# A graph kernel of two normalised layers: ten gather-free runs of tiles in place of nine in its second pass

## The chip, the cores and the metric

The kernel runs on one NeuronCore of a Trainium2 chip. The metric is the device time of one execution in microseconds (us), lower is better; it is given as the median of several runs.

The engines are called as in the profile: PE does matrix products (PEld is its weight load), DVE and ACT work on elements, POOL here only issues gathers (indirect DMAs), and SP issues the other DMAs. They run their own instruction lists in order and wait for each other by semaphores only.

## The reference

There are 6250 nodes with 128 features (`x`), 100000 edges sorted by destination (`src`, `dst`), an edge feature matrix `edge_attr` of 100000 x 128 and an edge weight. Cut to what matters:

```python
x = layernorm(x + sigmoid(gcn(relu(gcn(x, W1, b1)), W2, b2)))  # self-loops, symmetric norm
z, rh = x @ fc_w.T, edge_attr @ fc_r_w.T
e = leaky_relu(z[src] @ a0 + z[dst] @ a1 + rh @ a2)
alpha = segment_softmax(e, dst)
agg = segment_sum(alpha * (z[src] + rh), dst)
x = layernorm(x + relu(agg + z @ loop_w))
```

A `gcn` multiplies rows by a weight, gathers them by `src`, scales them per edge and sums them by `dst`.

## The kernel before

The edges lie in 782 tiles of 128 edges, in 98 groups of eight tiles. Since `dst` is sorted, the destinations of a tile fall into a window of 128 nodes. For a tile, POOL gathers the 128 source rows into a ring in on-chip memory (L720, one indirect DMA for each tile), DVE builds a matrix `S` that holds each edge's weight in the column of its destination (`build_S`, L1608), and PE multiplies rows by `S` and adds the product to a bank of accumulators (`sum_group`, L858). There are 17 banks of three 128-node blocks (`NA`); when the last group of a bank has been summed, ACT copies the bank out (L1215), PE multiplies it by the layer's weight (`layer`, L932), and DVE and ACT finish its nodes and store their rows for the next pass.

There are three passes over the edges: pass 0 (first GCN layer, reads `x1_d`), pass 1 (second GCN layer, reads `h1_d`) and pass 2 (attention, reads `x2_d`). The gathers of a pass can begin only when the last rows of the pass before are in memory (POOL waits for `h1_stored`, then for `x2_stored`). The ring has 18 places for groups in passes 0 and 1, so POOL can run up to 18 groups ahead of PE.

Some runs of 32 tiles have no gathers. The source rows of all nodes lie on chip anyway (`rows`, 49 blocks of 128). For such a set of 32 tiles the edges are sorted by source block once, in pass 0 (`make_hi`, `make_ranks`, `unpack` on DVE, `count_before`, `permute`, `turn_low` on PE, `store_low` on ACT). Then a run over the set goes through 49 buckets, one for each source block. ACT makes a one-hot of the source's place in its block (`slot_onehot`, L1239 and L1241), PE multiplies it by the block (`look_up`, L898), ACT copies the found rows (`copy_looked`, L1232), DVE builds a matrix of weights and destinations for each bucket (`make_slots`, L1682), and PE sums (`sum_slots`, L910). Four buckets make a chunk, so a run has 13 chunks (`NC`). At the end ACT copies the sum of the set (`copy_set`, L1256) and PE adds it to its bank (`add_sets`, L919).

Nine sets are sorted (`NSET`), one every six steps of pass 0 (`MAKE`). Pass 0 uses six of them, pass 1 all nine (`USED`). That leaves 74 groups (steps) with gathers in pass 0 and 62 in pass 1. The order of each engine's work is written out by hand per step: `CHUNK_AT` lists the step at which each chunk starts, `MAKE` that of each sort, `CLOSEH` the step at which each bank closes. In pass 1 a step of PE is: `look_up` for the chunks of the step before, `pick` (scores of the destinations, two groups in a step by `picks_at`), `add_sets`, `sum_group`, `sum_slots` for the same chunks, `layer`. A step of DVE is: `build_S`, `hidden2` of a bank closed two steps ago, `begin_pick`, `make_slots`, `residual`, then `normal`, `dst_scores` and `node_table` of a bank closed three steps ago. A step of ACT is: copies of the chunks, the copy of a finished set, one-hots for the chunks of the step, `squash` and `spread` of a bank (sigmoid and square root), the bank's copy. `residual` waits for `squash`. On SP's queue two steps before the end of pass 1 there stand four loads of `dlo_d` (L568), three of `edge_attr` (L505) and thirteen of `x2_d` (L574), and behind them the last three stores of `x2_d` (L603).

Of the kernel before, what the change touches and what calls it, by code (L numbers as in the profile page):

```python
# [12 lines left out]
P = 128  # L13
# [4 lines left out]
TC = G * GT  # L18
# [83 lines left out]
SETK = (6, 8, 10, 12, 14, 15, 2, 4, 9)  # L102
USED = ((0, 1, 2, 3, 4, 5), (6, 7, 0, 1, 8, 2, 3, 4, 5))
# [15 lines left out]
NQ = 15  # L119
assert all(bank_of(t0) == bank_of(t0 + ST - 1) == k and column(t0) + SPAN <= BW for k, t0 in zip(SETK, SAT))  # L120
CHUNK_AT = [[29 + m * 40 // (N0 * NC) for m in range(N0 * NC)], [1 + m * 57 // (len(USED[1]) * NC) for m in range(len(USED[1]) * NC)]]
MAKE = [17 + 6 * i for i in range(NSET)]
# [30 lines left out]
def picks_at(h):  # L153

    first = done = 0
    for i in range(h + 1):
        ready = sum(len(node_tiles(k)) // GT for k in range(NA) if CLOSEH[1][k] + 4 <= i)
        first, done = done, max(done, min(ready // 2 * 2, done + 2)) if i < HS[1] - 6 else done
    return range(first, done)
# [78 lines left out]
def build(nc, x, src, dst, edge_attr, edge_weight, W1, b1, W2, b2, fc_w, fc_r_w, attn_w, loop_w, out):  # L238
    ctx = ExitStack()
    with ctx:  # L240
# [61 lines left out]
        cols = sb("cols", [P, max(2 * TC + 2, 2 * SPAN + 2 * NSET * NB)])  # L302
        ewP = cols[:, 0:TC * 3 // 2].bitcast(BF16).rearrange("p (t k) -> p t k", k=3)
        eC, alC = cols[:, 0:TC + 2], cols[:, TC + 2:2 * TC + 2]
        setsum = cols[:, 0:2 * SPAN].rearrange("p (a n) -> p a n", a=2)
        slotD, slotW = (cols[:, 2 * SPAN + k * NSET * NB:2 * SPAN + (k + 1) * NSET * NB].rearrange("p (s a) -> p s a", a=NB) for k in range(2))
# [40 lines left out]
        Lb = sb("Lb", [P, 5, BW])  # L347
        aggT, u = Lb[:, 0:2], Lb[:, 2:4]
# [406 lines left out]
        def _(pe):  # L755
# [157 lines left out]
            def add_sets(p, h):  # L913
                for i in range(p * N0, p * N0 + len(USED[p])):
                    k = SETK[RUNS[i]]
                    if CLOSEH[p][k] == h:
                        pe.wait_ge(s("set_copied"), i + 1)
                        at = column(SAT[RUNS[i]])
                        nc.tensor.matmul(ps[(p * NA + k) % 2][:, at:at + SPAN], ident[:, :], setsum[:, i % 2, :], start=False, stop=False  # L919
                                         ).then_inc(s("set_added"), 1)  # L920
# [31 lines left out]
            for h in range(HS[0]):  # L952
                if h + 1 < R0:
                    lookup(h + 1)
                for s_, g in made_at(h, 2):
                    permute(s_, g)
                for m in chunks_at(0, h - 1):
                    look_up(m)
                for s_, g in made_at(h, 3):
                    if g == ST // GT - 1:  # L960
                        turn_low(s_)
                add_sets(0, h)
                sum_group(0, h)
# [212 lines left out]
        def _(act):  # L1176
# [74 lines left out]
            def copy_set(i):  # L1251
                act.wait_ge(s("slot_summed"), NB * (i + 1))
                if i >= 2:
                    act.wait_ge(s("set_added"), i - 1)
                at = act.value_load(shift[0:1, RUNS[i]:RUNS[i] + 1], min_val=0, max_val=SLACK)
                nc.scalar.copy(setsum[:, i % 2, :], ps[5][:, bass.ds(at, SPAN)]).then_inc(s("set_copied"), 1)  # L1256

            def set_copies(p, h):
                for m in chunks_at(p, h - 1):
                    copy_looked(m)  # L1260
                for m in chunks_at(p, h - 1):
                    if m % NC == NC - 1:
                        copy_set(m // NC)
# [10 lines left out]
            for h in range(HS[0]):  # L1274
                set_copies(0, h)
                for m in chunks_at(0, h):
                    slot_onehot(m)
                for s_, g in made_at(h, 3):
# [21 lines left out]
            for h in range(HS[1]):  # L1300
                set_copies(1, h)
                for m in chunks_at(1, h):
                    slot_onehot(m)
# [160 lines left out]
        def _(dve):  # L1464
# [263 lines left out]
            for h in range(HS[0]):  # L1728
# [4 lines left out]
                for s_, g in made_at(h, 0):  # L1733
                    make_hi(s_, g)
# [4 lines left out]
                for m in chunks_at(0, h):  # L1739
                    make_slots(m)  # L1740
                for s_, g in made_at(h, 2):
                    if g == ST // GT - 1:
                        unpack(s_)
                for k in range(NA):
                    if CLOSEH[0][k] == h - 2:
                        hidden(k)
# [96 lines left out]
            link(v.tensor_scalar(later, iota[:, 0:16], sd[:, 0:1], None, ALU.is_gt))  # L1843
            for h in range(HS[1]):
                build_S(1, h, ewC)
# [11 lines left out]
                for k in range(NA):  # L1857
                    if CLOSEH[1][k] == h - 2:
                        residual(k)
                    if CLOSEH[1][k] == h - 3 and k < NA - 3:  # L1860
                        normal(k)
                        dst_scores(k)
                        node_table(k)
# [11 lines left out]
            for i in range(REST, G // 2):  # L1875
                for k in (NA - 3, NA - 2, NA - 1):
# [385 lines left out]
```

## Time and profile before

| | us |
|---|---|
| median of 3 runs | 2372.62 (2370.83 to 2375.32) |
| the profiled execution's own time | 2381.5 |
| its span in the trace | 2379.7 |
| mean granted clock of TensorE | 0.88 of full speed |
| busy over the span: PE, DVE, POOL, ACT | 77%, 76%, 74%, 40% |

The span is what the trace covers; the profiled execution took 1.8 us more than it, and 8.9 us more than the median. In the trace the first gather of pass 1 starts at 788.76 us, the first of pass 2 at 1439.09 us. Shares over the whole span mix stages with different limits, so the rows below are cut by stage. The time of a gather on POOL is that of its issue; its landing is a DMA.

### The profile page before, as it was taken

To read this page: it belongs to the slowest core of one execution; us is meant where nothing else is said; L and a number is where in the kernel's file an instruction comes from. 1 tells how busy PE (TensorE), PEld (TensorE's weight loads), DVE (VectorE), ACT (ScalarE), POOL (GpSimd) and SP (SyncE) were. 2 spreads that over 40 slices of the span, in tenths; PEclk is the share of its full clock that TensorE was granted. 3 is DMA by queue.
4 is the path that set the end of the run, shared out by engine and by line. 5 is a ranking of instruction groups with operands and counts; after the bars stand their busy time and mean duration, and the time that the engine had idled before them with its cause. 6 is when DMAs were issued, how large, how long until landed. Compare 5 with 4: busy or idle time off the path is not lost.

```text
span 2379.7 us, 40822 instructions
## 1 busy us (share of the span) xinstructions
PE 1827.2 (77%) x13384; PEld 1615.7 (68%) x13384; DVE 1816.9 (76%) x7005; ACT 946.1 (40%) x1754; POOL 1756.1 (74%) x1781
## 2 busy tenths in 40 slices
PE   5657869999998588888889873477776779668976
PEld 4557758788887467777777762467665668657866
DVE  7989979999997356878878857486565876486686
ACT  5740024343432244354454431115562367226721
POOL 7777777777777677777777766777777777777771
PEclk9878889999999799999999985778897889779988
DMA  5243223332333333444545467534455555545550
GB/s 145 60 131 98 60 67 80 81 80 73 83 84 102 95 81 100 123 128 118 137 116 147 141 161 203 140 96 127 117 132 143 131 128 139 142 125 145 132 138 20
DMA packets 272093, 270.54 MB, mean 114 GB/s; under 512 B 43454, under 2 KB 218709, under 8 KB 271862
## 3 DMA queue, kind: packets, MB, share of 16 engines
q1 hardware_dynamic: 201790, 143.87, 21.5%
q0 software_dynamic: 56640, 117.52, 20.7%
q10 hardware_dynamic: 13448, 6.47, 1.0%
q8 instruction: 112, 1.84, 0.3%
q14 instruction: 103, 0.84, 0.1%
HBM read 254.14 MB, written 13.97 MB: 113 GB/s over the span
## 4 chain that ended last, share of the span: by engine, by line
POOL 42%; issue 19%; DVE 18%; PE 11%; DMA 6%; ACT 2%; SPq 2%; ACTq 0%; DVEq 0%; POOLq 0%
POOL ring L720 42%; DVE SR L1608 4%; DVE SR L1571 4%; PE ps L858 3%; DMA ring<-x_d,srcC 2%; PE ps L910 2%; DMA ring<-h_d,srcC 2%; PE ps L860 1%; DVE U L1710 1%; DMA ring<-in_edge_attr_dram 1%; PE ps L898 1%; PE ps L1045 1%; DVE SR L1682 1%; DVE U L1972 0%; SPq L574 0%
## 5 line engine op out<-in xcount | busy, mean ns | idle before, releaser
L720 POOL DMA_INDIRECT ring<-x_d,srcC x1132 | 1130.8, 999 | 369.0 <-issue 359.1
L858 PE MATMUL ps<-SR,ring 128*128 128x128 f32 x3540 | 615.3, 305 | 132.9 <-DVE SR L1608 59.4
L858 PEld LDWEIGHTS ps<-SR,ring 128*128 128x128 f32 x3540 | 536.3, 218 | 158.7 <-issue 94.6
L720 POOL DMA_INDIRECT ring<-h_d,srcC x494 | 477.9, 968 | 158.0 <-issue 153.7
L1682 DVE TENSOR_SCALAR SR<-iota_r,cols 128x288 f32<-128x288 f32 x735 | 364.0, 562 | 62.4 <-PE ps L910 62.0
L910 PE MATMUL ps<-SR 128*128 128x288 f32 x1470 | 379.6, 411 | 0.0
L860 PE MATMUL ps<-SR 128*128 128x128 f32 x1564 | 321.4, 301 | 6.0 <-DVE SR L1608 6.0
L910 PEld LDWEIGHTS ps<-SR 128*128 128x128 f32 x1470 | 275.3, 193 | 71.7 <-issue 2.6
L1232 ACT COPY SR<-ps 128x512 f32<-128x512 f32 (+1 forms) x195 | 107.8, 561 | 473.8 <-PE ps L898 446.4
L860 PEld LDWEIGHTS ps<-SR 128*128 128x128 f32 x1564 | 264.0, 218 | 6.2 <-issue 6.1
L1608 DVE TENSOR_SCALAR SR<-iota,rankC,ewC 128x128 f32<-128x128 f32 x940 | 255.9, 365 | 2.2 <-DVE U L1814 0.6
L1608 DVE TENSOR_SCALAR SR<-iota,rankC,cols 128x128 f32<-128x128 f32 x782 | 209.9, 357 | 5.9 <-PE ps L860 4.3
L898 PE MATMUL ps<-rows,SR 128*128 128x128 f32 x1470 | 187.5, 280 | 17.6 <-ACT SR L1241 14.2
L898 PEld LDWEIGHTS ps<-rows,SR 128*128 128x128 f32 x1470 | 179.5, 195 | 25.6 <-ACT SR L1241 20.0
L720 POOL DMA_INDIRECT ring<-in_x_dram,srcC x144 | 145.4, 1010 | 46.8 <-issue 43.6
L1710 DVE SCALAR_TENSOR_TENSOR U<-SR,v2B 128x128 f32<-128x128 f32 x686 | 152.2, 285 | 6.8 <-DMA SR<-in_edge_attr_dram 5.3
L1239 ACT ACTIVATE SR<-SR,negp 128x512 bf16<-128x512 bf16 (+1 forms) x195 | 134.7, 691 | 27.4 <-PE ps L898 16.9
L1241 ACT ACTIVATE SR<-SR,negp 128x512 f32<-128x512 bf16 (+1 forms) x195 | 136.0, 697 | 6.3
L1919 DVE TENSOR_TENSOR cols<-ring,s1C 128x32 f32<-128x32 f32 (+6 forms) x31 | 5.3, 190 | 149.5 <-DMA ring<-x_d,srcC 149.0
L995 PE MATMUL ps<-ident,cols 128*32 128x128 f32 (+2 forms) x81 | 18.2, 350 | 126.6 <-DVE cols L1922 110.1
L792 PE MATMUL ps<-iota_r,zero_h 1*128 1x512 bf16 (+1 forms) x128 | 50.6, 417 | 72.2 <-DMA ring<-h_d,srcC 22.6
L1352 ACT ACTIVATE U<-U 32x384 f32<-32x384 f32 (+2 forms) x27 | 14.1, 523 | 227.9 <-DVE U L1967 227.7
(288 smaller groups left out, 2716.8 us busy)
## 6 DMA issues: line engine op xcount, KB each, us to landing
SR<-in_edge_attr_dram SPq DMA_DIRECT2D x97, 512.0 KB, 4.1
SR<-low_d SPq DMA_DIRECT2D x90, 256.0 KB
U<-dlo_d SPq DMA_DIRECT2D x74, 256.0 KB
ring<-x_d,srcC POOLq DMA_INDIRECT x1132
ring<-h_d,srcC POOLq DMA_INDIRECT x494
SR<-dlo_d SPq DMA_DIRECT2D x12, 512.0 KB, 6.0
ring<-in_edge_attr_dram SPq DMA_DIRECT2D x12, 512.0 KB
U<-lo_d SPq DMA_DIRECT2D x18, 256.0 KB
```

The costliest lines, as they stand in the source:

```text
L720: pool.indirect_dma_start(ring[:, ring_at(p, h if p < 2 else q), k, 0:width], None, (x if p == 0 and h < R0 else table)[:, :], bass.Indire ...
L858: last = nc.tensor.matmul(ps[(p * NA + k) % 2][:, at], ring[:, ring_at(p, h), j, 0:D], S[:, gg % NS, j, :], start=False, stop=stop)
L860: last = nc.tensor.matmul(ps[2 + k % 2][:, at], rh[:, q % NR, j, :], S[:, gg % NS, j, :], start=False, stop=stop)
L898: last = nc.tensor.matmul(ps[3 + m % 2][:, i * P:(i + 1) * P], ohS[:, m % 2, i * P:(i + 1) * P], rows[:, a, 0:D], start=True, stop=True)
L910: nc.tensor.matmul(ps[5][:, SLACK:SPAN], rowX[:, m % 2, i * P:(i + 1) * P], slotS[:, n % NQ, :], start=False, stop=a == NB - 1).then_inc(s ...
L1232: nc.scalar.copy(rowX[:, m % 2, 0:n], ps[3 + m % 2][:, 0:n]).then_inc(s("looked_copied"), 1)
L1239: nc.scalar.activation(low, low, ACT.Abs, bias=negp[:, 0:1]).then_inc(s("low_apart"), 1)
L1241: return nc.scalar.activation(out, low, ACT.Relu, bias=negp[:, 1:2], scale=-1.0)
L1571: last = v.tensor_scalar(SH[:, q % ND, j, :], iota_h[:, :], rankC[:, t:t + 1], None, ALU.is_equal)
L1608: last = v.tensor_scalar(S[:, gg % NS, j, :], iota[:, :], rankC[:, t:t + 1], w[:, t:t + 1], ALU.is_equal, ALU.mult)
L1682: v.tensor_scalar(slotS[:, n % NQ, :], iota_up, slotD[:, RUNS[i], a:a + 1], slotW[:, RUNS[i], a:a + 1], ALU.is_equal, ALU.mult).then_inc(s ...
L1710: v.scalar_tensor_tensor(junk[:, n % NJ, :], attr, 1.0, v2B[:, :], ALU.mult, ALU.mult, accum_out=s2C[:, t:t + 1]).then_inc(s("rh_dotted"), 1)
```

## The change

Pass 1 runs ten sets without gathers in place of nine; a tenth set is therefore sorted in pass 0, and the sorts follow each other every 5 or 6 steps. Pass 1 then has 58 steps with gathers in place of 62, and its 130 chunks start at `1 + m*5//12` in place of 117 at `1 + m*57//117`. The one-hots for a chunk's lookup are made right behind the copy of the chunk two before it, and no longer behind the copy of a finished set. In pass 1 DVE builds `S` one step ahead. In pass 0 DVE's order within a step changes, and a set's last transposition and store come a step earlier. The ring of bucket matrices has 16 places in place of 15; the second buffer of the set sums moves to `Lb`, for which its first use waits on a store of `dlo_d`. Where more than 12 groups of picks are due, four are done in a step; 35 pairs of picks in place of 36 fall into pass 1, and the node table of bank 13 moves behind the pass.

```diff
-SETK = (6, 8, 10, 12, 14, 15, 2, 4, 9)
-USED = ((0, 1, 2, 3, 4, 5), (6, 7, 0, 1, 8, 2, 3, 4, 5))
+SETK = (6, 8, 10, 12, 14, 15, 2, 3, 4, 11)
+USED = ((0, 1, 2, 3, 4, 5), (6, 7, 8, 0, 1, 2, 9, 3, 4, 5))
-NQ = 15
+NQ = 16
-CHUNK_AT = [[29 + m * 40 // (N0 * NC) for m in range(N0 * NC)], [1 + m * 57 // (len(USED[1]) * NC) for m in range(len(USED[1]) * NC)]]
-MAKE = [17 + 6 * i for i in range(NSET)]
+CHUNK_AT = [[29 + m * 40 // (N0 * NC) for m in range(N0 * NC)], [1 + m * 5 // 12 for m in range(len(USED[1]) * NC)]]
+MAKE = [17 + 11 * i // 2 for i in range(NSET)]
...
-        first, done = done, max(done, min(ready // 2 * 2, done + 2)) if i < HS[1] - 6 else done
+        first, done = done, max(done, min(ready // 2 * 2, done + (4 if ready - done > 12 else 2))) if i < HS[1] - 6 else done
...
+        setsum = (cols[:, 0:SPAN], Lb[:, 4, P:P + SPAN])
...
-                for s_, g in made_at(h, 3):
+                add_sets(0, h)
+                sum_group(0, h)
+                for s_, g in made_at(h, 2):
                     if g == ST // GT - 1:
                         turn_low(s_)
-                add_sets(0, h)
-                sum_group(0, h)
...
+                if i == 1:
+                    act.wait_ge(s("dlo_stored"), 16)
...
                 for m in chunks_at(p, h - 1):
                     copy_looked(m)
+                    if m + 2 < (len(RUNS) if p else N0) * NC:
+                        slot_onehot(m + 2)
...
             for h in range(HS[1]):
                 set_copies(1, h)
-                for m in chunks_at(1, h):
-                    slot_onehot(m)
+                if h == CHUNK_AT[1][0]:
+                    slot_onehot(N0 * NC)
+                    slot_onehot(N0 * NC + 1)
...
+            build_S(1, 0, ewC)
             for h in range(HS[1]):
-                build_S(1, h, ewC)
+                if h + 1 < HS[1]:
+                    build_S(1, h + 1, ewC)
...
-                        node_table(k)
+                        if k < NA - 4:
+                            node_table(k)
...
-                for k in (NA - 3, NA - 2, NA - 1):
+                for k in (NA - 4, NA - 3, NA - 2, NA - 1):
```

In pass 0 `make_hi` moves behind `build_S` and `make_ranks`, `make_slots` behind `unpack`, ACT's one-hots go the same way as in pass 1, and `store_low` follows `turn_low` to `made_at(h, 2)`.

## Rows read from the trace of the kernel before

**Rows 1.** Chain of waits by line from 787, 1195 and 1450 us on.

```profile
by line: POOL ring L720 64.1%; issue 27.7%; DMA ring<-h_d,srcC 8.9%; POOLq L719 0.0%
...
by line: PE ps L910 20.0%; PE ps L858 14.2%; PE ps L898 8.0%; DVE SR L1608 7.9%; DVE SR L1682 5.7%; issue 5.5%; SPq L505 4.1%; SPq L574 3.7%; ACT SR L1239 3.5%; DMA U<-dlo_d 2.5%; PE ps L840 2.4%; ACT L1293 1.7%; ACT SR L1241 1.6%; DVE U L1
...
by line: POOL ring L720 65.3%; issue 25.5%; DMA ring<-x_d,srcC 3.7%; PE ps L858 1.5%; PE ps L860 1.3%; PE ps L1020 0.9%; PE ps L995 0.3%; DVE U L1966 0.2%; DVE U L1972 0.2%; DVE U L1965 0.2%; PE ps L792 0.2%; PE ps L1077 0.1%; DVE U L1973 0
```

**Rows 2.** Busy us of PE, PEld, DVE, ACT, POOL (instructions); clock, DMA, GB/s.

```profile
400.00:500.00 100.00, 93.06 (x629) 81.08 (x630) 92.47 (x271) 41.12 (x71) 77.13 (x76) 0.98 0.31 79
...
787.00:1425.00 638.00, 526.96 (x3601) 458.25 (x3601) 477.48 (x1573) 280.67 (x441) 477.95 (x494) 0.93 0.45 122
```

**Rows 3.** Timeline of POOL: start, length, line, idle before it.

```profile
788.76 0.95 POOL L720 DMA_INDIRECT ring<-h_d,srcC  x1 [7.32 <-issue]
...
1416.41 0.95 POOL L720 DMA_INDIRECT ring<-h_d,srcC  x1 [0.31 <-issue]
1439.09 1.10 POOL L720 DMA_INDIRECT ring<-x_d,srcC  x1 [21.73 <-issue]
```

**Rows 4.** Groups of POOL, 400:700 and 900:1300 us: busy, mean ns, idle.

```profile
L720 POOL DMA_INDIRECT ring<-x_d,srcC x230 | 230.7, 1003 | 70.1 <-issue 67.7 <-DMA ring<-x_d,srcC 2.4
...
L720 POOL DMA_INDIRECT ring<-h_d,srcC x314 | 305.5, 973 | 95.8 <-issue 93.6 <-DMA ring<-h_d,srcC 2.1
```

**Rows 5.** Waits of PE, 787:1425 us: total us, times, longest.

```profile
PE ps L858 <- DVE SR L1608: 32.1, 17, 3.5
PE ps L792 <- DMA ring<-h_d,srcC: 22.6, 5, 14.7
PE ps L858 <- DMA ring<-h_d,srcC: 21.4, 13, 5.2
PE ps L792 <- DVE SR L1608: 15.1, 6, 6.7
PE ps L898 <- ACT SR L1241: 12.0, 9, 2.6
...
PE ps L898 <- ACT SR L1232: 3.3, 3, 1.3
```

**Rows 6.** Columns as rows 2: PE L910, L898, L858, DVE L1682, L1608 alone.

```profile
787.00:1425.00 638.00, 228.54 (x882) 166.23 (x882) 0.93 0.45 122
...
787.00:1425.00 638.00, 112.38 (x882) 108.96 (x882) 0.93 0.45 122
...
787.00:1425.00 638.00, 145.12 (x988) 136.00 (x988) 0.93 0.45 122
...
787.00:1425.00 638.00, 218.74 (x441) 0.93 0.45 122
...
787.00:1425.00 638.00, 133.84 (x494) 0.93 0.45 122
```

**Rows 7.** Timeline of PE at three moments of pass 1.

```profile
1017.39 1.13 PE L898 MATMUL ps<-rows,SR 128*128 128x128 f32 x8 [1.22 <-ACT SR L1232]
...
1346.67 3.64 PE L858 MATMUL ps<-SR,ring 128*128 128x128 f32 x16 [3.49 <-DVE SR L1608]
...
1374.39 2.03 PE L858 MATMUL ps<-SR,ring 128*128 128x128 f32 x16
```

**Rows 8.** Groups of the sorts on DVE and PE, 290:787 us.

```profile
L1649 DVE TENSOR_SCALAR U<-iota,U 128x128 f32<-128x128 f32 x248 | 52.1, 298 | 4.6 <-PE ps L885 4.2
L1637 DVE TENSOR_REDUCE U<-U 128x49 f32<-128x392 bf16 x23 | 24.4, 1061 | 0.8
...
L1635 DVE TENSOR_REDUCE U<-U 128x8 f32<-128x392 f32 x30 | 16.8, 561 | 1.0
...
L885 PE MATMUL ps<-U 128*128 128x98 f32 x498 | 62.2, 279 | 0.7 <-DVE U L1651 0.6
```

**Rows 9.** End of pass 1: timeline of the SP queue and DVE.

```profile
1427.71 9.38 SPq L603 DMA_DIRECT2D x_d<-U  x3
...
1432.65 0.35 DVE L1757 SCALAR_TENSOR_TENSOR U<-ps,dinv,b2B 128x128 f32<-128x128 f32 x1 [7.46 <-DMA x_d<-U]
```

More of the change, by code:

```diff
@@ L301, in build @@
         wraw = s1C[:, 0:R0 * GT]
-        cols = sb("cols", [P, max(2 * TC + 2, 2 * SPAN + 2 * NSET * NB)])
+        cols = sb("cols", [P, max(2 * TC + 2, SPAN + 2 * NSET * NB)])
         ewP = cols[:, 0:TC * 3 // 2].bitcast(BF16).rearrange("p (t k) -> p t k", k=3)
         eC, alC = cols[:, 0:TC + 2], cols[:, TC + 2:2 * TC + 2]
-        setsum = cols[:, 0:2 * SPAN].rearrange("p (a n) -> p a n", a=2)
-        slotD, slotW = (cols[:, 2 * SPAN + k * NSET * NB:2 * SPAN + (k + 1) * NSET * NB].rearrange("p (s a) -> p s a", a=NB) for k in range(2))
+        slotD, slotW = (cols[:, SPAN + k * NSET * NB:SPAN + (k + 1) * NSET * NB].rearrange("p (s a) -> p s a", a=NB) for k in range(2))
         U = sb("U", [P, 4648])
@@ L918, in add_sets @@
                         at = column(SAT[RUNS[i]])
-                        nc.tensor.matmul(ps[(p * NA + k) % 2][:, at:at + SPAN], ident[:, :], setsum[:, i % 2, :], start=False, stop=False
+                        nc.tensor.matmul(ps[(p * NA + k) % 2][:, at:at + SPAN], ident[:, :], setsum[i % 2], start=False, stop=False
                                          ).then_inc(s("set_added"), 1)
@@ L1254, in copy_set @@
                     act.wait_ge(s("set_added"), i - 1)
+                if i == 1:
+                    act.wait_ge(s("dlo_stored"), 16)
                 at = act.value_load(shift[0:1, RUNS[i]:RUNS[i] + 1], min_val=0, max_val=SLACK)
-                nc.scalar.copy(setsum[:, i % 2, :], ps[5][:, bass.ds(at, SPAN)]).then_inc(s("set_copied"), 1)
+                nc.scalar.copy(setsum[i % 2], ps[5][:, bass.ds(at, SPAN)]).then_inc(s("set_copied"), 1)
             def set_copies(p, h):
@@ L1275, in _ @@
                 set_copies(0, h)
-                for m in chunks_at(0, h):
-                    slot_onehot(m)
-                for s_, g in made_at(h, 3):
+                if h == CHUNK_AT[0][0]:
+                    slot_onehot(0)
+                    slot_onehot(1)
+                for s_, g in made_at(h, 2):
                     if g == ST // GT - 1:
@@ L1301, in _ @@
                 set_copies(1, h)
-                for m in chunks_at(1, h):
-                    slot_onehot(m)
+                if h == CHUNK_AT[1][0]:
+                    slot_onehot(N0 * NC)
+                    slot_onehot(N0 * NC + 1)
                 for k in range(NA - 2):
@@ L1732, in _ @@
                     select(h)
-                for s_, g in made_at(h, 0):
-                    make_hi(s_, g)
                 for i in ([h] if h < R0 else []) + ([h + 1] if R0 <= h + 1 < HS[0] else []):
@@ L1738, in _ @@
                     make_ranks(s_, g)
-                for m in chunks_at(0, h):
-                    make_slots(m)
+                for s_, g in made_at(h, 0):
+                    make_hi(s_, g)
                 for s_, g in made_at(h, 2):
@@ L1743, in _ @@
                         unpack(s_)
+                for m in chunks_at(0, h):
+                    make_slots(m)
                 for k in range(NA):
```

## The prediction, made before the changed kernel was run

> **What bounds the kernel now.** I read the chain of waits by stage first, since each pass can begin only when the one before has stored its rows. From 787 to 1195 us POOL's gathers and the gaps between their issues fill the chain (64.1% and 27.7%); from 1195 to 1425 us PE's sums and lookups and DVE's matrices take it over; from 1450 us on POOL holds it again [rows 1]. So pass 1, the stage that the change is about, has two masters: the gathers, and in its second half a coupled step of PE, DVE and ACT.
>
> The busy times show why this can be: over the 638 us of pass 1 PE is busy 527, DVE 477.5, POOL 478 and ACT 281 us [rows 2]. None is full. POOL's list is simple: its gathers run from 788.76 to 1417.36 us, and 494 of them are recorded, so one takes 628.6/494 = 1.2725 us, issue gap included [rows 3]. Before them POOL waits for nothing but its own issue and 2.1 us of landings [rows 4]: it never waits for a place in the ring. So POOL's time in pass 1 is the count of gathers times 1.27 us. After the last gather come 21.7 us until pass 2's first [rows 3].
>
> PE's waits complete the picture. It waits 44.0 us for gathers (22.6 + 21.4), 47.2 us for `S` (32.1 + 15.1), and 15.3 us for one-hots and copies in front of lookups (12.0 + 3.3) [rows 5]. With the 527 busy that makes 633.5 of 638; five us are small waits. The 44 us are all that PE has in hand against POOL.
>
> **The change, part by part.** *Gathers.* Four groups of eight tiles fewer: 32 x 1.2725 = 40.7 us less on POOL.
>
> *What replaces them.* Per bucket PE spends 228.54/441 = 0.518 us on the sum and 112.38/441 = 0.255 us on the lookup (two instructions each, 882 recorded); a gathered tile costs it 145.12/494 = 0.294 us [rows 6]. So PE gets 49 x 0.773 = 37.9 us more and 32 x 0.294 = 9.4 us less: +28.5 us, to 555.5. DVE gets 49 x 218.74/441 = 24.3 us of bucket matrices and loses 32 x 133.84/494 = 8.7 us of `S`: +15.6, to 493 of some 597 us. ACT can't get more than its whole 281 us shared over 117 chunks, times 13: 31 us, to 312. DVE and ACT keep room; PE is the one to watch.
>
> *The moved orders.* With `S` built a step ahead, DVE no longer has it behind `residual`, which waits for a sigmoid; of PE's 47.2 us nothing to all may go. I take 37 us, since DVE keeps 100 us of room, but a bank closes every two steps at 12 to 18 and 40 to 46, where DVE will run late. What is late next is `make_slots`; the place of PE that waits for it is the sum, which in the rows of before waits for nothing. One-hots no longer stand behind `copy_set`, which waits for the last sum of a set. Against that, chunks now start 2.4 per step: 22 steps take three, in place of three steps before. The third lookup needs a one-hot and a copy that are only made in the same step; in such a step before it waited 1.22 us [rows 7]. I take 22 x 1.22 = 27 us for all waits of lookups. Below, it is 0, where PE would have waited for gathers anyway; above, each costs the longest one-hot wait, 2.6 us [rows 5], together 57.
>
> *The clock.* A group's sum took 2.03 us in a run of uninterrupted work and 3.64 us right behind a wait of 3.49 us [rows 7], and the granted clock was 0.93 over pass 1, but 0.98 in a stretch of pass 0 where PE was 93% busy [rows 2]. Fewer waits should give back some of that: 555.5 us at 0.93 is 538 at 0.96, my value; the bounds are 527 (at 0.98) and 555.5.
>
> *PE's account.* 538 busy + 10 for `S` + 27 for lookups + 5 small = 580 us. POOL's: 638 - 40.7 = 597. So POOL remains the bound by 17 us on average; stretches in which PE falls behind are carried by the ring, and the last two steps have no chunks, in which PE catches up.
>
> *The tenth sort, in pass 0.* Per group of eight tiles DVE makes eight L1649 of 52.1/248 = 0.21 us, five operations like L1635 of 0.56 us, and in three of four groups one L1637 of 1.06 us: 5.3 us; four groups and some 18 small ones of about 0.2 us (estimate) give 25 us. PE multiplies 16 x 62.2/498 = 2.0 us per group, 8 us per set, and counts, which I bound by as much again: at most 16 us [rows 8]. Pass 0 keeps its 592 gathers. Where pass 0 is densest, DVE is busy 92.5 and PE 93.1 of 100 us [rows 2]. A set every 5.5 steps and not 6 raises the sorts' load by a ninth of a sixth: per step DVE 25/5.5 - 25/6 = 0.4 us, PE 0.2, with a step of eight gathers at 1.31 us, 10.5 us [rows 4]. That is 96% and 95%: still under POOL, and the last steps of pass 0 have no chunks. If this cover were gone, DVE's 25 us less the 7.5% of room over some 40 steps would put about 10 us on the path. One price remains: gathers there take 1.31 us, and 1.28 in pass 1 [rows 4]. If the nine sets of sorts make these 0.03 us over some 430 gathers, a tenth costs 1.4 us. For pass 1, with DVE busier, I add 1 us in the same way (0 to 14: 464 gathers times 0.03).
>
> *Costed at nothing:* the new place of `setsum` (what it waits for is done long before the second run ends), one more small load in the setup, the earlier `turn_low` and `store_low`, the changed order of pass 0 and the 16th bucket matrix. They add waits on things done steps before; ACT's `store_low` has one late copy behind it, within a step of 10.5 us. The pair of picks and the node table that move behind pass 1 are DVE work of some 4 us where POOL holds the chain [rows 1].
>
> *The end of pass 1.* SP's queue issues twenty loads before the last three stores, which begin at 1427.71 us; DVE waits 7.46 us for one of them [rows 9]. All these steps keep their distance from the last group, so the 21.7 us stay. They would be 14 without that wait, and about 32 if PE ends a step late. I add 2 us for a PE that is later than before.
>
> **Sum.** -40.7 + 1.4 + 1 + 2 = -36.3 us. The profiled execution's 2381.5 us become 2345.2. It lay 8.9 us over the median, so the median should be 2336.
>
> **A rule against it.** The busiest gathers of pass 0 took 1003 ns with DVE 92% busy, those of pass 1 973 ns with DVE less busy [rows 2, 4]: 3% between them. The Trainium skill (SBUF — State Buffer, "Who interferes with whom") says that `tensor_scalar` and copies can enter a mode in which they hold a port pair that GpSimd shares, and that GpSimd then stands still for the whole instruction; by that rule what is added on DVE would be added to the gathers. The trace bears out little of it.
>
> **The rivals.** *PE sets the pace* of pass 1: half of the waits for `S` stay and the clock doesn't recover. 555.5 + 24 + 27 + 5 = 612 in place of 638: -26, and with the 3.4 us of the other terms 2350. For it speaks that PE led the chain from 1195 us [rows 1]; against it that the change unhooks just the waits of that stretch. *DVE bounds pass 0*: 10 us more, 2346; its 92.5% speak for it, the late steps without chunks against. *DVE holds up the gathers*: every added us of bucket matrices and sorts, 15.6 + 25 = 40.6, stands in POOL's way. That eats the 40.7: no change, 2372; the 3% above speak against it. *Slower:* the third lookup of a step. If no wait for `S` goes and each of the 22 steps waits 2 us, PE needs 555.5 + 47 + 44 + 5 = 652, 14 us over today's 638: 2387. It decides from (638 - 555.5 - 47 - 5)/22 = 1.4 us per step on, if nothing else gets better; the 1.22 us are near that, but the waits for `S` would have to stay whole.
>
> **How the numbers follow.** Chances: the sum as it stands 0.62, PE sets the pace 0.22, DVE bounds pass 0 0.06, gathers held up 0.04, slower 0.06. So 0.90 for faster by over 0.2% (about what a measurement of this kernel can tell from no change), 0.04 for the same, 0.06 for slower. The likeliest case has 2328 (all 40.7 us, and 4 of the end's wait) to 2345 (PE ends a step late). The range goes on to 2356, the pace-setting PE with 6 us more. That leaves out the same, the slower, and the worse third of the second case: under 2 in 10.
>
> **What would show it.** Right: 464 gathers in pass 1 at 1.27 to 1.28 us; first gather of pass 1 within 3 us of 788.8, of pass 2 near 1403; waits of PE for L1608 near 10 us; waits before L898 near 27 us; from pass 2's first gather to the end as now, 940.6 us. Wrong: POOL waiting for PE (then the ring was full), waits of PE before L910, or a gap from last gather to pass 2 well over 22 us (PE sets the pace); a later 788.8 (DVE in pass 0); gathers at 1.30 us or more (held up). A shorter pass 2 would be a gain that I have no term for.

## The result, and the profile after

The changed kernel takes 2415.35 us (median of 4 runs, 2408.34 to 2418.38), the kernel before beside it 2373.97 (2370.83 to 2375.65). The ratio is 1.0169, 95% interval 1.0152 to 1.0185: slower by 1.7%. The forecast was 2336, faster. The profiled execution took 2418.1 us, with a span of 2416.2.

POOL did what the prediction asked of it. Its timeline (start, length, line, idle before), to be read against [rows 3]:

```profile
800.30 0.94 POOL L720 DMA_INDIRECT ring<-h_d,srcC  x1 [18.98 <-issue]
...
1383.15 0.94 POOL L720 DMA_INDIRECT ring<-h_d,srcC  x1 [0.30 <-issue]
1477.90 1.11 POOL L720 DMA_INDIRECT ring<-x_d,srcC  x1 [93.81 <-issue]
```

The gathers of pass 1 now take 582.9 us from the first to the last, where they took 627.7. But then POOL stands for 93.81 us, in place of 21.73, until pass 2's table is stored. Add up the stages: pass 1 begins 11.5 us later (800.30 against 788.76), lasts 27.3 us longer from its first gather to pass 2's first (677.6 against 650.3), and the rest is 2.3 us shorter (938.3 against 940.6): +36.5 us, the difference of the two spans. The time was lost in the stages that were to gain it. In pass 0 the gathers themselves were not late: the last one ends at 781.32 us, against 781.44 before, and the 11.5 us are the idle time behind it, 18.98 us in place of 7.32 [rows 3].

Who holds pass 1 now is seen in the chain of waits by line, from 800 us on (cut off by the view at its end; beside it the first line of [rows 1]): POOL is down to 6.5%, and PE leads.

```profile
by line: PE ps L910 26.0%; PE ps L858 12.8%; PE ps L898 10.5%; DVE SR L1688 8.9%; issue 6.9%; POOL ring L720 6.5%; DMA U<-dlo_d 3.2%; DVE SR L1614 2.8%; ACT SR L1239 2.7%; ACT SR L1241 2.4%; PE ps L840 1.8%; PE ps L944 1.6%; DMA ring<-h_d,s
```

The busy times by stretch (columns of [rows 2]) and PE's waits in pass 1 (total us, times, longest; beside [rows 5]) give its account:

```profile
400.00:500.00 100.00, 97.42 (x679) 85.09 (x678) 94.65 (x283) 41.95 (x75) 76.63 (x77) 1.00 0.32 82
800.00:1465.00 665.00, 556.27 (x3720) 481.58 (x3720) 491.84 (x1577) 302.27 (x482) 443.00 (x462) 0.92 0.43 116
```

```profile
PE ps L898 <- ACT SR L1241: 51.0, 22, 8.1
PE ps L792 <- DMA ring<-h_d,srcC: 15.7, 1, 15.7
PE ps L944 <- DVE s1C L1842: 13.2, 2, 6.9
PE ps L858 <- DMA ring<-h_d,srcC: 10.4, 4, 5.0
PE ps L792 <- ACT cols L1258: 6.2, 3, 2.8
PE ps L792 <- ACT Lb L1258: 6.0, 3, 2.6
PE ps L792 <- ACT Lb L1215: 1.6, 1, 1.6
PE ps L792 <- ACT SR L1232: 0.8, 1, 0.8
```

`build_S` (now L1614) is gone from the list: its 47.2 us have become 0. In its place stand 51.0 us in front of lookups (L898), 22 waits, one for each step of three chunks. The line of the last matrix product of pass 1 ends at 1458.3 us, so PE needs 658.0 us from the first gather, and 19.6 us more pass until pass 2 can start.

Where do the waits come from? Take the longest, on the timelines of three engines (start, length, line, idle before). ACT:

```profile
1331.63 1.28 ACT L1303 ACT_TABLE_LOAD   x1
1339.29 0.30 ACT L1303 ACTIVATE sd<-mv,epsc 128x3 f32<-128x3 f32 x1 [6.37 <-DVE mv L1776]
1339.49 0.57 ACT L1215 COPY Lb<-ps 128x512 f32<-128x512 f32 x1
1339.96 0.59 ACT L1232 COPY SR<-ps 128x512 f32<-128x512 f32 x1
1340.43 0.73 ACT L1239 ACTIVATE SR<-SR,negp 128x512 bf16<-128x512 bf16 x1
1341.20 0.72 ACT L1241 ACTIVATE SR<-SR,negp 128x512 f32<-128x512 bf16 x1
```

DVE and PE at the same time:

```profile
1331.88 5.85 DVE L1688 TENSOR_SCALAR SR<-iota_r,cols 128x288 f32<-128x288 f32 x12
...
1338.94 0.31 DVE L1776 BATCH_NORM_AGGREGATE mv<-bst 128x2 f32<-128x6 f32 x3
```

```profile
1331.98 1.95 PE L898 MATMUL ps<-rows,SR 128*128 128x128 f32 x16
1341.98 2.07 PE L898 MATMUL ps<-rows,SR 128*128 128x128 f32 x8 [8.05 <-ACT SR L1241]
```

Read it backwards. PE has done two lookups by 1334 and waits 8.05 us for the third one's one-hot. ACT makes that (L1239, L1241) only behind the copy of the step's first lookup (L1232), and before this copy it stood 6.37 us at `spread`, a square root of 0.30 us. `spread` waits for a bank's statistics, which DVE takes behind three chunks' bucket matrices (12 of L1688, 5.85 us). The copy of the first lookup, which was done by 1334, begins only after `spread`, at 1339.96. The Trainium skill (Perfetto Trace Analysis, section "Tensor Engine Instruction (MATMUL, LD_WEIGHTS)") says in a note that ACT and DVE take instructions strictly in order; the trace agrees with these two times. Five of the 22 waits lie at a `spread` (4.69, 5.89, 5.78, 8.05 and 4.47 us, together 28.9). In four of them ACT stands idle in it for 4.1 to 6.4 us; in the one of 5.78 us it is idle for only 1.10, and the rest is what stands ahead of it: the copy of a finished set, the sigmoid and two table loads of 1.28 us. The other 17 waits are short, 22.1 us in all.

Pass 0 has its own answer in PE's waits, 290 to 798 us. Where PE had waited 43.0 us for gathers in that stage, it now waits 7.4; it stands at `turn_low` (L891) until DVE has unpacked a sorted set. The first two rows are of the kernel before (290 to 787 us), the others of the change:

```profile
PE ps L858 <- DMA ring<-x_d,srcC: 31.1, 12, 6.7
PE ps L792 <- DMA ring<-x_d,srcC: 11.9, 4, 6.4
...
PE ps L891 <- DVE U L1667: 27.9, 8, 6.1
PE ps L870 <- DVE U L1633: 7.5, 5, 3.1
PE ps L858 <- DMA ring<-x_d,srcC: 5.3, 2, 3.8
...
PE ps L792 <- DMA ring<-x_d,srcC: 2.1, 1, 2.1
```

### The profile page after: what moved, and what is told of

It is laid out like the page before. It is cut to its first block, busy times and chain, and to the rows that moved or that the text cites. A ratio compares the mean times of both kernels' runs of the same rounds, so it can differ in the third digit from the quotient of the medians.

```text
span 2416.2 us, 41469 instructions
## 1 busy us (share of the span) xinstructions
PE 1869.3 (77%) x13620; PEld 1648.1 (68%) x13620; DVE 1859.1 (77%) x7100; ACT 965.2 (40%) x1795; POOL 1720.5 (71%) x1749
## 4 chain that ended last, share of the span: by engine, by line
PE 28%; DVE 27%; POOL 23%; issue 11%; DMA 5%; ACT 4%; SPq 1%; ACTq 0%; DVEq 0%; POOLq 0%
POOL ring L720 23%; PE ps L910 11%; PE ps L858 6%; DVE SR L1688 5%; DVE SR L1614 5%; DVE SR L1577 4%; PE ps L898 4%; DMA ring<-x_d,srcC 2%; DVE U L1655 1%; DVE U L1716 1%; PE ps L885 1%; PE ps L860 1%; DMA ring<-in_edge_attr_dram 1%; DMA U<-dlo_d 1%; ACT SR L1239 1%
## 5 line engine op out<-in xcount | busy, mean ns | idle before, releaser
L858 PE MATMUL ps<-SR,ring 128*128 128x128 f32 x3476 | 589.1, 299 | 62.6 <-DVE SR L1614 27.1
L858 PEld LDWEIGHTS ps<-SR,ring 128*128 128x128 f32 x3476 | 514.0, 213 | 82.1 <-issue 55.7
L720 POOL DMA_INDIRECT ring<-h_d,srcC x462 | 443.0, 959 | 159.8 <-issue 151.9
L1688 DVE TENSOR_SCALAR SR<-iota_r,cols 128x288 f32<-128x288 f32 x784 | 386.6, 561 | 79.8 <-PE ps L910 79.3
L910 PE MATMUL ps<-SR 128*128 128x288 f32 x1568 | 418.7, 422 | 0.0
L910 PEld LDWEIGHTS ps<-SR 128*128 128x128 f32 x1568 | 302.3, 198 | 82.2 <-issue 2.8
L1232 ACT COPY SR<-ps 128x512 f32<-128x512 f32 (+1 forms) x208 | 114.9, 553 | 505.5 <-PE ps L898 402.1
L860 PEld LDWEIGHTS ps<-SR 128*128 128x128 f32 x1564 | 261.4, 216 | 6.2 <-issue 6.1
L1614 DVE TENSOR_SCALAR SR<-iota,rankC,ewC 128x128 f32<-128x128 f32 x908 | 246.7, 365 | 2.1 <-DVE U L1820 0.8
L898 PE MATMUL ps<-rows,SR 128*128 128x128 f32 x1568 | 203.0, 282 | 51.0 <-ACT SR L1241 51.0
L898 PEld LDWEIGHTS ps<-rows,SR 128*128 128x128 f32 x1568 | 193.3, 197 | 59.8 <-ACT SR L1241 55.2
L1614 DVE TENSOR_SCALAR SR<-iota,rankC,cols 128x128 f32<-128x128 f32 x782 | 209.9, 357 | 5.6 <-PE ps L860 4.3
L1239 ACT ACTIVATE SR<-SR,negp 128x512 bf16<-128x512 bf16 (+1 forms) x208 | 145.7, 701 | 11.4 <-DMA SR<-low_d 11.0
L1241 ACT ACTIVATE SR<-SR,negp 128x512 f32<-128x512 bf16 (+1 forms) x208 | 145.4, 699 | 6.8
L1577 DVE TENSOR_SCALAR SR<-iota_h,rankC 128x128 bf16<-128x128 bf16 x584 | 97.9, 290 | 0.2
```

The costliest lines, as they stand in the source:

```text
L720: pool.indirect_dma_start(ring[:, ring_at(p, h if p < 2 else q), k, 0:width], None, (x if p == 0 and h < R0 else table)[:, :], bass.Indire ...
L858: last = nc.tensor.matmul(ps[(p * NA + k) % 2][:, at], ring[:, ring_at(p, h), j, 0:D], S[:, gg % NS, j, :], start=False, stop=stop)
L860: last = nc.tensor.matmul(ps[2 + k % 2][:, at], rh[:, q % NR, j, :], S[:, gg % NS, j, :], start=False, stop=stop)
L898: last = nc.tensor.matmul(ps[3 + m % 2][:, i * P:(i + 1) * P], ohS[:, m % 2, i * P:(i + 1) * P], rows[:, a, 0:D], start=True, stop=True)
L910: nc.tensor.matmul(ps[5][:, SLACK:SPAN], rowX[:, m % 2, i * P:(i + 1) * P], slotS[:, n % NQ, :], start=False, stop=a == NB - 1).then_inc(s ...
L1232: nc.scalar.copy(rowX[:, m % 2, 0:n], ps[3 + m % 2][:, 0:n]).then_inc(s("looked_copied"), 1)
```

## The experiments

The table has, of each kernel's profiled execution, the first gather of pass 1, the length of pass 1 up to pass 2's first gather, and PE's waits in front of L898 in pass 1; then the median and its ratio to the kernel before, measured beside it (2373.97 to 2375.20 us), with the 95% interval.

```
kernel                       first gather  pass 1   L898    median   ratio
before                          788.76     650.3    15.3    2373.97  1
the change                      800.30     677.6    51.0    2415.35  1.0169 [1.0152, 1.0185]
e1 nine sets                    793.94     650.3     4.1    2379.09  1.0020 [1.0007, 1.0032]
e2 ten sets, old orders         817.92     736.7    68.1    2497.77  1.0531 [1.0503, 1.0558]
e3 turn_low late                794.16     676.3    52.3    2409.60  1.0156 [1.0133, 1.0179]
e4 before, turn_low early       787.41     650.7    14.4    2374.15  1.0001 [0.9989, 1.0014]
e5 spread later                 798.50     654.7    27.6    2390.53  1.0063 [1.0039, 1.0087]
e6 third lookup later           796.47     644.7    18.2    2381.97  1.0031 [1.0019, 1.0043]
e7 e5 and e6                    795.60     636.0     0.8    2373.64  0.9988 [0.9973, 1.0004]
e8 S not ahead                  794.86     697.5    36.4    2435.64  1.0258 [1.0226, 1.0291]
e9 e7 and e3                    792.65     630.7     0.8    2365.27  0.9964 [0.9947, 0.9981]
e10 e9, loads last              793.39     621.5     0.7    2356.04  0.9922 [0.9905, 0.9939]
e11 before, loads last          785.15     641.7    15.1    2366.55  0.9969 [0.9958, 0.9980]
e12 e1, e5 and e6               787.87     647.7     0.0    2379.92  1.0032 [1.0005, 1.0059]
```

**Which part costs: the tenth run or the moved orders?** First the changed kernel with the nine sets and their steps of before, all moved orders kept:

```diff
-SETK = (6, 8, 10, 12, 14, 15, 2, 3, 4, 11)
+SETK = (6, 8, 10, 12, 14, 15, 2, 4, 9)
-USED = (..., (6, 7, 8, 0, 1, 2, 9, 3, 4, 5))
+USED = (..., (6, 7, 0, 1, 8, 2, 3, 4, 5))
-CHUNK_AT = [..., [1 + m * 5 // 12 ...]]
+CHUNK_AT = [..., [1 + m * 57 // (len(USED[1]) * NC) ...]]
-MAKE = [17 + 11 * i // 2 for i in range(NSET)]
+MAKE = [17 + 6 * i for i in range(NSET)]
```

> The changed kernel with nine sets again (the sets, their use, the chunk steps and the six-step sorts of before), all its moved orders kept. Theory A (the tenth run makes PE the bound of pass 1: more sums, and third lookups that wait on ACT; the moved orders by themselves are no loss there): pass 1 lasts about 650 us from first gather to pass 2's first, as before or up to 10 us less, PE's waits for S near 0; in all 2360 to 2380. Theory B (the moved orders are what is slow, the tenth run alone would gain its 40 us): pass 1 over 665 us, in all 2395 to 2425.

Measured: 2379.09 us, pass 1 650.3 us as before. PE's waits for S were 2.3 us, and its waits for gathers had grown from 44.0 to 87.1: with nine runs the gathers set the pace, and what the orders save PE is no gain.

Then the reverse, the kernel before with the ten sets, their steps and buffers, and with the early `turn_low` that sets after 5 steps need, but the other orders of before. In it part of the sorted payload of some sets is overwritten by the next set's, so that part of the sums runs over other values; the amount of work is the same.

```diff
-SETK = (6, 8, 10, 12, 14, 15, 2, 4, 9)
+SETK = (6, 8, 10, 12, 14, 15, 2, 3, 4, 11)
-NQ = 15
+NQ = 16
-MAKE = [17 + 6 * i for i in range(NSET)]
+MAKE = [17 + 11 * i // 2 for i in range(NSET)]
...
```

> The kernel before with ten sets, their sorts, chunks, picks and buffers as in the change, and the early transposition of a set, without which it would deadlock; S, one-hots, node table and the order of DVE in pass 0 as before. Theory A: slower than the changed kernel, since PE's waits for S come back (30 to 47 us) beside its longer list: 2420 to 2460. Theory B: faster than before, 2330 to 2345.

Measured: 2497.77 us, 38 us over the top of theory A's range. The waits for `S` came back with 26.7 us, fewer than expected, but the waits for lookups rose to 68.1, and pass 1 began 17.6 us later than in the change. So the moved orders are worth 82 us to ten sets and, by e1, nothing to nine: they repair a part of what the tenth run does to PE. Next `S` alone, built in its own step again:

```diff
-            build_S(1, 0, ewC)
             for h in range(HS[1]):
-                if h + 1 < HS[1]:
-                    build_S(1, h + 1, ewC)
+                build_S(1, h, ewC)
```

> The changed kernel, with S built in its own step as before and not one step ahead; all else as changed. Theory A (TensorE's waits add to its pace): the waits before L858 and L792 for S come back, 40 to 60 us of them, and the whole goes to 2440 or more. Rival (S ahead is worth nothing, since TensorE waits for the lookup's one-hots in the same steps): within 6 us of 2415.

Measured: 2435.64 us, a little under theory A's 2440, pass 1 19.9 us longer than in the change. The waits for `S` came back with 29.5 us, fewer than the 40 to 60 expected, and the waits for lookups fell to 36.4, perhaps since DVE and ACT had more time meanwhile:

```profile
PE ps L898 <- ACT SR L1241: 36.4, 22, 5.1
PE ps L858 <- DVE SR L1614: 17.5, 10, 5.2
...
PE ps L792 <- DVE SR L1614: 12.0, 5, 4.6
```

So `S` ahead is worth 20 us of the whole: the step of the prediction that counted on it holds, but a part of what it frees is taken by the next wait.

**Is it the lookups' waits?** One edit for each of the two kinds. `spread` a step later, behind the next step's copies and one-hots:

```diff
             for h in range(HS[1]):
                 set_copies(1, h)
...
+                for k in range(NA - 2):
+                    if CLOSEH[1][k] == h - 3:
+                        spread(k)
                 for k in range(NA - 2):
                     if CLOSEH[1][k] == h - 2:
                         squash(k)
-                        spread(k)
```

> The changed kernel, with ScalarE's square root of a bank's variance (spread) taken one step later, behind the next step's copies and one-hots. Theory A (TensorE sets the pace of pass 1, and five of its 22 waits in front of lookups are long, 4.5 to 8 us, because ScalarE stands at spread until VectorE's bucket matrices and statistics are through): the long waits, 28.9 us together, shrink to about 1.2 us each, the waits before L898 go from 51 to about 28 us, pass 1 from first gather to first gather of pass 2 goes from 677.6 to about 655, the whole to about 2392 (2385 to 2400). Theory B (TensorE is slowed by its work and clock alone, and a wait removed there comes back in front of the bucket sums or of the gathers): waits before L898 shrink, others grow by as much, the whole stays within 5 us of 2415.

Measured: 2390.53 us, pass 1 654.7, waits before L898 27.6 us and none longer than 3.1. Theory A gave 2392, 655 and 28. And the third lookup of a step behind the group's sum:

```diff
-                for m in chunks_at(1, h - 1):
+                for m in chunks_at(1, h - 1)[:2]:
                     look_up(m)
                 for q in picks_at(h - 1):
                     pick(q)
                 add_sets(1, h)
                 sum_group(1, h)
+                for m in chunks_at(1, h - 1)[2:]:
+                    look_up(m)
```

> The changed kernel, with the third lookup of a step issued behind the group's sum and not straight behind the second lookup. Theory A: the 17 ordinary waits of 1.16 us go whole, the five long ones lose about 2 us each, together 51 to about 21 us; pass 1 becomes some 30 us shorter, the whole about 2385 (2378 to 2395). Theory B: within 5 us of 2415, with waits before L910 or L858 in their place.

Measured: 2381.97 us, six waits left, 18.2 us (21 expected). Theory B fell in both. Then both edits at once:

```diff
-                        spread(k)
...
-                for m in chunks_at(1, h - 1):
+                for m in chunks_at(1, h - 1)[:2]:
...
```

> Both edits of the two runs before. Theory A: hardly any wait before L898 is left (under 5 us), TensorE has 556 us of work and some 45 us of other waits (the first gather, the copies of finished sets, the end), pass 1 is 620 to 632 us and the whole 2362 to 2375: about the kernel before, with pass 0 still 11 us longer than there. Theory B: over 2400.

Measured: 2373.64 us, pass 1 636.0 us, a little over the 620 to 632. PE has less work than expected (538.7 us and not 556) and more other waits (78.9 us and not 45). The changed kernel is level with the kernel before again. Its busy row over the same 3720 matrix products, and PE's waits from 800 to 1420 us:

```profile
800.00:1420.00 620.00, 538.66 (x3720) 467.94 (x3720) 484.20 (x1559) 302.43 (x482) 441.96 (x459) 0.93 0.45 124
```

```profile
PE ps L792 <- DMA ring<-h_d,srcC: 20.7, 2, 16.0
PE ps L944 <- DVE s1C L1849: 19.1, 2, 10.4
PE ps L858 <- DMA ring<-h_d,srcC: 13.8, 5, 4.9
PE ps L944 <- DVE U L1840: 7.4, 7, 2.8
PE ps L792 <- ACT cols L1260: 6.2, 3, 2.8
PE ps L792 <- ACT Lb L1260: 6.0, 3, 2.6
PE ps L792 <- ACT Lb L1217: 5.0, 1, 5.0
PE ps L898 <- ACT SR L1243: 0.8, 1, 0.8
```

PE's last product of pass 1 ends at 1410.3 us, 614.7 us after the first gather, while POOL is through at 1381.6: PE is still the bound (in the kernel before, its last product ends 6.8 us after POOL's last gather, here 28.7). The rest of its waits is not about lookups. Of it, the 19.1 us at L944 stand in two places, as in the change (13.2 us): they are the two steps, 22 and 50, in which the change does four picks and not two, and PE waits there for DVE ahead of the second pair. In the change the second of them is

```profile
1398.62 0.57 PE L944 MATMUL ps<-U 128*128 128x3 bf16 x16 [6.95 <-DVE s1C L1842]
```

No run takes this order back, so what it costs the whole is not shown.

A control, the two edits with nine sets:

```diff
-SETK = (6, 8, 10, 12, 14, 15, 2, 3, 4, 11)
+SETK = (6, 8, 10, 12, 14, 15, 2, 4, 9)
...
-                        spread(k)
...
-                for m in chunks_at(1, h - 1):
+                for m in chunks_at(1, h - 1)[:2]:
...
```

> Nine sets with all moved orders of the change (the run with nine sets) and both edits for the lookups. Theory A (with nine sets the gathers set the pace of pass 1, so TensorE's waits cost nothing there): pass 1 stays at 650 us and the whole within 5 us of the 2379 without the edits. Rival (the two edits are worth 40 us for any number of sets): 2340 to 2350.

Measured: 2379.92 us (1.0032, interval 1.0005 to 1.0059), the same as without them, as theory A had it. What PE no longer waits for lookups it waits for gathers:

```profile
PE ps L858 <- DMA ring<-h_d,srcC: 57.0, 28, 7.0
PE ps L792 <- DMA ring<-h_d,srcC: 21.5, 11, 4.6
```

**Pass 0.** The change with `turn_low` at the head of PE's step and `store_low` ahead of the copies, one step later, for all sets but the last:

```diff
+                for s_, g in made_at(h, 3):
+                    if g == ST // GT - 1 and s_ + 1 < NSET:
+                        turn_low(s_)
                 for s_, g in made_at(h, 2):
                     permute(s_, g)
...
                 for s_, g in made_at(h, 2):
-                    if g == ST // GT - 1:
+                    if g == ST // GT - 1 and s_ + 1 == NSET:
                         turn_low(s_)
```

> The changed kernel with the transposition and store of a sorted set a step later and at the start of the step (all sets but the last). Theory A0 (in pass 0 the early transposition makes PE wait for DVE's unpack, 27.9 us, and that is the 11.5 us by which pass 1 starts later): first gather of pass 1 at 788 to 793 us and 8 to 11 us off the total. Theory B0 (DVE's 25 us for the tenth sort are what lengthens pass 0): first gather of pass 1 stays at 797 to 802 us and the total moves by under 3 us.

And the kernel before with the early `turn_low`, `store_low` and `unpack` of the change:

```diff
-                for s_, g in made_at(h, 3):
-                    if g == ST // GT - 1:
-                        turn_low(s_)
                 add_sets(0, h)
                 sum_group(0, h)
+                for s_, g in made_at(h, 2):
+                    if g == ST // GT - 1:
+                        turn_low(s_)
```

> The kernel before, nine sets, with only the transposition and store of a set a step earlier (and unpack ahead of the bucket matrices on DVE, which it needs). Theory A0: PE waits 10 to 28 us for unpack, and pass 1 starts 0 to 8 us later than 788.8. Theory B0: no such wait of over 5 us, and pass 1 starts within 1 us of 788.8.

Measured: 2409.6 and 2374.15 us. With nine sets the early transposition costs nothing: PE waits 0.5 us for `unpack`, where theory A0 had 10 to 28, and pass 1 starts 1.4 us earlier than in the kernel before. With ten neither theory came out as stated (a start at 794.16 us, 5.8 us off the total), and the interval of the whole overlaps the change's; the starts of pass 1 over all runs say more. The change, e5, e6, e7 and e8 have the same pass 0 and start pass 1 at 794.86 to 800.30 us, mean 797.1. With the late transposition it is 792.65 to 794.16 (e3, e9, e10), mean 793.4. The kernel before and e4 and e11 have 785.15 to 788.76, mean 787.1. So on these means pass 0 is 10 us longer with the change, of which the late transposition gives back 3.7. That is not the tenth sort alone: e1 and e12, nine sets with the moved orders of pass 0, start at 793.94 and 787.87 us, and these two have the same pass 0.

The idle time of POOL between its last gather of pass 0 and its first of pass 1 scatters less. It is 7.0 to 7.7 us in all five kernels with nine sets, 9.3 to 19.0 us (mean 13.2) in the change, e5, e6, e7 and e8, 40.1 in e2, and 8.6 to 9.8 us (mean 9.1) in the three with the late transposition. The rest of the differences is when the last gather ends, and that is 777.9 to 786.3 us with nine sets and 777.8 (e2) to 786.3 with ten. So with ten sets PE and DVE end pass 0 late, and the late transposition takes most of that away. Put together with e7:

```diff
-                        spread(k)
...
-                for m in chunks_at(1, h - 1):
+                for m in chunks_at(1, h - 1)[:2]:
...
+                    if g == ST // GT - 1 and s_ + 1 < NSET:
+                        turn_low(s_)
...
```

> The changed kernel with both edits for the lookups (spread a step later, third lookup behind the group's sum) and the late transposition: turn_low and store_low of all sets but the last one step later, ahead of that step's work. If TensorE's 24 us of waits for unpack in front of turn_low are what made pass 0 longer (pass 1 begins at 795 to 800 us in place of 789), they go, pass 1 begins near 789 and the whole is 6 us under the run with both edits, about 2367 (2362 to 2371). If VectorE has too much work in pass 0 in any case, pass 1 begins at 794 or later and the whole is 2371 to 2376.

Measured: 2365.27 us, ratio 0.9964 (0.9947 to 0.9981); in pass 0 its waits for `unpack` are gone and 25.0 us of waits for gathers are back, yet pass 1 starts at 792.65 and not at 789:

```profile
792.65 0.94 POOL L720 DMA_INDIRECT ring<-h_d,srcC  x1 [8.81 <-issue]
```

**The end of pass 1.** In e7 SP's queue and DVE show what comes after PE's last sum:

```profile
1402.79 7.24 SPq L505 DMA_DIRECT2D SR<-in_edge_attr_dram  x3
1410.12 9.98 SPq L574 DMA_DIRECT2D rows<-x_d  x13
1420.15 0.34 SPq L555 DMA_DIRECT2D U<-in_x_dram  x1
1420.54 8.99 SPq L603 DMA_DIRECT2D x_d<-U  x3
```

```profile
1425.08 0.35 DVE L1770 SCALAR_TENSOR_TENSOR U<-ps,dinv,b2B 128x128 f32<-128x128 f32 x1 [12.94 <-DMA x_d<-U]
```

The last three stores of pass 1's result stand behind 16 loads that only pass 2 needs, and DVE waits 12.94 us for one of them. The loads were put behind the stores, in e9's kernel and in the kernel before:

```diff
                 if h + 2 == HS[1]:
...
-                    for d in range(3):
-                        load_rh(d, d)
-                    sp.wait_ge(s("looked"), len(RUNS) * NC)
-                    for k in range(NA - 4):
-                        load_x2(k)
...
+            for d in range(3):
+                load_rh(d, d)
+            sp.wait_ge(s("looked"), len(RUNS) * NC)
+            for k in range(NA - 4):
+                load_x2(k)
             for i in range(REST + 1 + NP_DLO, G // 2):
                 load_pair(i)
```

> The run before, and SyncE's loads of pass 2 (three groups of edge rows, 13 banks of node rows) issued behind the last three stores of pass 1 and not ahead of them. In the run with both edits they took SyncE's queue from 1402.8 to 1420.1 us, while VectorE waited 12.9 us for the store of the third last bank: if that queue sets the end of pass 1, pass 2's first gather comes some 13 us earlier and the whole is about 2355 (2350 to 2360). If the late loads are missed at the start of pass 2, the gain is given back there: over 2362.

> The kernel before, with the same edit of SyncE's loads alone. There VectorE waited 7.46 us for that store, and 21.7 us lay between the last gather of pass 1 and the first of pass 2. If the queue sets the end: 14 us in place of 21.7, the whole 2367 (2364 to 2370). If the loads are missed later: 2372 or more.

Measured: 2356.04 us, ratio 0.9922 (0.9905 to 0.9939), and 2366.55, ratio 0.9969 (0.9958 to 0.9980). In the first the step saves 9.2 us of the 13 expected: from PE's last product of pass 1 to pass 2's first gather it is 8.6 us in place of 20.9, but PE's products took 4.4 us longer. In the second the gap before pass 2 goes from 21.73 to 15.25 us. e10 beats both kernels. Of the 19 us that it lies under the kernel before (2375.20 beside it), e11 has 8.7 without the tenth run; 10.5 us are left for ten sets with all their orders.

## Why the prediction was wrong

**Gathers: right.** 462 of 464 gathers are recorded in pass 1, at 1.26 us with the issue gap, against 1.2725 before. POOL was done with pass 1 at 1384, three us from where the sum had it (1403 less the 21.7), in part by luck: it began 10 us later than forecast and took 583.8 us, 5 us less than the 588.9 of the sum (628.6 - 40.7 + 1). The 40.7 us were saved, on an engine that no longer set the end.

**Gathers held up: no.** A gather took 0.959 us between 900 and 1300 us, against 0.973 [rows 4]. Pass 1 alone is a weak test, since DVE was busy for about the same share of it (491.84 of 665 us, 477.48 of 638). Pass 0 is a better one: from 290 to 775 us DVE had 445.94 us of work in place of 427.42, and 372 gathers took 371.86 us where 373 had taken 371.58. The Trainium skill (SBUF — State Buffer, "Who interferes with whom") says that a DVE instruction in a two-port mode and GpSimd (POOL here) shut each other out for the whole instruction. By that rule, as the prediction put it, the 18.5 us should have been added to the gathers; the runs here show none of it, and whether any of these instructions entered such a mode they don't show.

**PE's account: the step that failed.** It had 580 us, under POOL's 597. By terms, with e7 for what became of them:

```
term                            predicted   the change   e7
matrix products                     538        556.3     538.7
waits for S                          10          0         0
waits in front of lookups            27         51.0       0.8
waits for gathers                     0         26.1      34.5
clear behind copy_set (L1258)         -         12.2      12.2
picks (L944)                          -         13.2      26.5
small ones                            5          3.1       5.7
sum                                 580        661.9     618.4
```

(PE's own span, 658.0 and 614.7 us, is some 4 us under the sums.) Four terms carry the miss of 82 us, against which the waits for `S` gave 10 more than forecast:

- *Lookups, +24.* The mechanism was named, the third lookup of a step, and also its count of 22. But I priced each at 1.22 us, a wait of the kernel before in which no `spread` stood between. 17 waits came out near that, 1.3 us; five were 4.5 to 8 us, since ACT came late out of `spread`, four times for DVE's statistics. e5 shortened the five to 3.1 us and less, e6 took the 17 away but for one, and the time went with them: 25 and 33 us of the whole, 42 together. A wait that was taken out of one queue (`S` behind `residual`) came back through another engine's.
- *The clock, +18.* The 555.5 us without a recovery were right to a microsecond: the forecast took fewer waits for granted, and PE's waits hardly changed (105.6 us, against 111.4 before). e7, with 79.7 us of waits, has 538.7 for the same 3720 products, but at a granted clock of 0.93 and not at the 0.96 of the sum, so that its match with 538 is not the sum's working come true.
- *Waits for gathers, +26.* I struck all 44 us as room. But 14.7 of them [rows 5] were PE's wait for the first gather of the pass, which no slack elsewhere removes; it is 15.7 now. That row was at hand. Another 10.4 us of waits for gathers stayed further on.
- *The small ones, +23.* The clear of the accumulator (L792) waits for `copy_set` when a set ends inside a step, 12.2 us in six waits (3.8 in three before): the new `CHUNK_AT` makes it happen twice as often. Picks wait for DVE, 13.2, in the two steps that do four of them. I had costed `setsum` at nothing for its new place, looked at no wait for its copy, and had no term for the four picks on PE.

**`S`: right**, and more than asked: 47.2 us went to 0, not to 10. **Pass 0:** +1.4 us was expected and +10 came (11.5 in the profiled execution). The nearest rival is "DVE bounds pass 0", which I gave 0.06 and priced at 10 us, but that price was luck: 7.5% of room over 40 steps of 10.5 us is 31.5 us, more than the 25 us that it was to hold, so the working gives nothing on the path. Nor was DVE shown as the bound: where it was busy 94.65 of 100 us, PE was busy 97.42. PE stands behind `unpack`, and 3.7 us of the 10 come back when `turn_low` stands a step later. So the line "costed at nothing" for the earlier `turn_low` failed too. Of what is left, some 2 us are still idle time of POOL behind its last gather of pass 0 (9.1 us with the late transposition, 7.4 with nine sets); the remainder lies in when that gather ends, which differs by 8 us among the kernels with nine sets too, so the runs don't tell what it is due to. **The end:** the loads ahead of the last stores were named rightly and e11 shows their price. **The signs:** the later start and the long gap before pass 2 (93.81 us) came, the waits before L910 did not, and POOL waited only 1.2 us for PE. **The rivals:** "PE sets the pace" is what happened, but at 2415 and not 2350; "slower" had the right place, but its condition, that the waits for `S` stay whole, wasn't needed: other waits did the same.

## What to carry to other kernels

When work is moved from one engine to another, give the receiving engine an account of its own from the first input of the stage to its last output, and put every wait that it has today into it, the first input's landing too; only what the giving engine causes, and all along the stage, may be struck. In a step that several engines share in strict order, follow the longest thing that stands ahead of each instruction on *its* engine: a 0.3 us square root that stood between a copy and its lookup, and mostly waited for another engine, came with five waits of 4.5 to 8 us. And a change that is slower may be a right change half done: two moved calls brought back 42 us.

## What was unexpected of the hardware

The time of the same 3720 matrix products of pass 1 went with PE's waits: 538.7 us in e7, 556.3 in the change, 561.9 in e8 and 575.2 in e2, where PE's waits in that stage add up to 79.7, 105.6, 118.9 and 146.2 us; the granted clock was 0.93, 0.92, 0.92 and 0.89. In these kernels a wait of PE thus went with more loss than its own length: e7 takes away 50 us of waits for lookups, and 17.6 us of work go with them (25.9 us of waits in all: those for gathers and picks grew). No run changes the waits alone, and the sum of the waits is not all of it: the five kernels with nine sets have 104.3 to 111.4 us of them, and their 3601 products took 527.0 to 533.8 us, the least where PE waited most. Pass 0, which is the same in five of the kernels, began pass 1 at any time from 794.86 to 800.30 us, so that a difference of a few us in one stage of a single execution says little here.
